# One opening block: setup, first norm and weight turns interleaved, and later weight loads held back behind wqk0

## The chip, the cores and the metric

The kernel runs on one core of a Trainium2 chip. The metric is the device time of one execution, in microseconds, as the median of several runs. A profiled execution of the same kernel gives the trace from which rows are read; "span" is the time from its first to its last instruction.

## What is computed

Four layers are applied to `x` (4 batches, 256 tokens, 128 features), each conditioned on one vector per batch. Layer 0, cut to what the change touches:

```python
mod = silu(c) @ W_mod + b_mod                 # six vectors of 128 per batch
sh_msa, sc_msa, g_msa, sh_mlp, sc_mlp, g_mlp = split(mod, 6)
h = layernorm(x) * (1 + sc_msa) + sh_msa
q, k, v = split(h @ W_qkv, 3)                 # 16 heads of 64
x = x + g_msa * (softmax(q k^T / 8) v @ W_out + b_out)
x = x + g_mlp * (gelu((layernorm(x) * (1 + sc_mlp) + sh_mlp) @ W1 + b1) @ W2 + b2)
```

Layer 1 is a graph attention over the edge tensor `adj`, layers 2 and 3 are attention blocks of 16 heads of 8 with modulated norms; layer 3 has an MLP. Activations are held transposed (features on the partitions), so a norm turns `x` with TensorE into token form, takes its statistics there, and turns it back.

## The kernel before

**The order of the work.** A planner at the top of the file writes a list of steps. Each step holds "heavy" ticks (`gv`: q, k and v of a batch in layer 0; `attention`) and "light" ticks (norms, projections, MLPs, layer 1). Every engine walks that one list in its own instruction stream, so the order on each engine is fixed when the kernel is built, and semaphores hold it where a producer is late. The list begins with the eight ticks of `norm 0a` of batch 0; then `gv` of batch 0 begins beside `norm 0a` of batch 1, and a step later attention of batch 0.

**Two blocks.** Ahead of the walk stands a block of setup (L504 to L584). SyncE (SP) issues every load of the beginning in one queue (L507 to L519): `vec`, the modulation columns of `w0`, `x` of batch 0, the two halves of `wqk0` (q and k weights, 512 KB each, into the tile `room`), `x` of batches 1 to 3, the rest of `w0`, `wbias`, `w1`, `w2`, `w3`, `bv2`. GpSimd (POOL) makes the identity and small constants (L531 to L538). ScalarE (ACT) and VectorE (DVE) form silu of the condition (L543, L558 to L560), TensorE (PE) multiplies it with the modulation columns (L583), and DVE makes the modulation vectors from that (L562 to L575). `vec` and the modulation columns share the semaphore `first_in`, so silu waits for both. All engines meet at the end of this block before the second one begins.

**The start of the second block.** SP goes on with the loads of `adj` (L702, L704). POOL makes the masks and zeroed tiles (L869 to L898) before it walks the list. PE turns `x` of batch 0 (L1378), DVE takes the statistics (L1075, L1079), ACT forms the reciprocal deviation (L908, L911), DVE normalizes (L1085), PE turns back (L1387) and ACT modulates into `hT` (L921). Then, in `gv` of batch 0, PE turns the 16 pieces of `wqk0` in four parts (L1397), ACT copies parts 0 and 2 out of PSUM (L928) and DVE parts 1 and 3 (L1104); two PSUM banks alternate. With all four copied, PE makes q and k of two heads at a time (L1406, "a G pair" below: two float32 matmuls, four matmul records), DVE copies them to `big` (L1111), ACT casts them to `room` (L933), and the scores follow (L1455). The v products (L1416) need the rest of `w0`; the late modulations (L1581) need `w1` to `w3` and `bv2`; the edge work on DVE (L1241) needs `adj`.

Of the kernel before, what the change touches and what calls it, by code (L numbers as in the profile page):

```python
# [383 lines left out]
def cond_seq_kernel(nc, x_t, adj, w0, wqk0, w1, w2, w3, wp2, wproj3, vecs, rows, out_t):  # L384
    with ExitStack() as ctx:
# [93 lines left out]
        first_in = sem("first_in")  # L479
# [13 lines left out]
        mods_full = sem("mods_full")  # L493
        w_full = sem("w_full")
# [5 lines left out]


        with nc.Block() as block:
            @block.sync
            def _(sp):  # L504

                mod0 = slice(*W0_AT["mod"])
                sp.dma_start(vec[:], vecs).then_inc(first_in, 16)  # L507
                sp.dma_start(w0s[:, mod0], w0[:, mod0]).then_inc(first_in, 16)
                sp.dma_start(xT[:, 0, :], x_t[0]).then_inc(x_loaded[0], 16)
                for s in range(2):  # L510
                    sp.dma_start(wqk0s[s * DH0:(s + 1) * DH0], wqk0[:, s]).then_inc(wqk_in, 16)
                for b in range(1, B):
                    sp.dma_start(xT[:, b, :], x_t[b]).then_inc(x_loaded[b], 16)
                sp.dma_start(w0s[:, mod0.stop:], w0[:, mod0.stop:]).then_inc(w0_in, 16)
                sp.dma_start(wbias[:], rows[0:1, D:D + NL + 1].broadcast_to([128, NL + 1])).then_inc(wbias_in, 16)
                sp.dma_start(w1s[:], w1).then_inc(weights_in, 16)
                sp.dma_start(w2s[:], w2).then_inc(weights_in, 16)
                sp.dma_start(w3s[:], w3).then_inc(weights_in, 16)
                sp.dma_start(bv2[:], rows[0:1, 0:D].broadcast_to([128, D])).then_inc(weights_in, 16)  # L519

            @block.gpsimd
            def _(pool):
                done = [0]

                def step(ins):

                    done[0] += 1
                    ins.then_inc(consts_step, 1)
                    pool.wait_ge(consts_step, done[0])

                step(nc.gpsimd.memset(ident[:], 0.0))  # L531
                step(nc.gpsimd.affine_select(out=ident[:], in_=ident[:], compare_op=ALU.not_equal, fill=1.0, base=0,
                                             pattern=[[-1, 128]], channel_multiplier=1))
                nc.gpsimd.tensor_copy(identb[:], ident[:]).then_inc(consts, 1)
                nc.gpsimd.memset(zero[:], 0.0)
                nc.gpsimd.memset(eps[:], EPS)
                nc.gpsimd.memset(lnd[:], -0.5 * math.log(D))
                nc.gpsimd.memset(ones[:], 1.0).then_inc(consts, 1)  # L538

            @block.scalar  # L540
            def _(act):
                act.wait_ge(first_in, 32)
                nc.scalar.activation(silu[:, 0, :], col(0, "cond", 0, B), ACT.Exp, scale=-1.0).then_inc(act_exp_c, 1)  # L543

            @block.vector
            def _(dve):
                done = [0]

                def step(ins):

                    done[0] += 1
                    ins.then_inc(setup_step, 1)
                    dve.wait_ge(setup_step, done[0])

                dve.wait_ge(first_in, 32)
                dve.wait_ge(act_exp_c, 1)

                step(nc.vector.tensor_scalar(silu[:, 1, :], silu[:, 0, :], 1.0, None, ALU.add))  # L558
                step(nc.vector.reciprocal(silu[:, 2, :], silu[:, 1, :]))
                nc.vector.tensor_tensor(silu[:, 0, :], silu[:, 2, :], col(0, "cond", 0, B), ALU.mult).then_inc(silu_ready, 1)  # L560
                dve.wait_ge(mods_full, 1)
                step(nc.vector.tensor_tensor(raw[:, 0:6, :], psum[:, 2, 0:6 * B].rearrange("p (c b) -> p c b", b=B),  # L562
                                             col(0, "mods", 0, 6).unsqueeze(2).broadcast_to([128, 6, B]), ALU.add))

                def block_mods(base, sc, sh, gate, bias):

                    nc.vector.tensor_scalar(mods_all[:, base, :], raw[:, sc, :], 1.0, None, ALU.add)
                    nc.vector.tensor_copy(mods_all[:, base + 1, :], raw[:, sh, :])
                    nc.vector.tensor_copy(mods_all[:, base + 2, :], raw[:, gate, :])
                    step(nc.vector.tensor_scalar(mods_all[:, base + 3, :], raw[:, gate, :], bias, None, ALU.mult))  # L570

                block_mods(SC0A, 1, 0, 2, col(0, "b_out0"))
                block_mods(SC0B, 4, 3, 5, col(0, "b2_0"))
                nc.vector.tensor_scalar(bq1s[:], col(0, "bq1", 0, 2), float(DH) ** -0.5, None, ALU.mult)
                nc.vector.tensor_tensor(bout1[:], col(0, "bout1", 0), col(0, "bout1", 1), ALU.add)  # L575

            @block.tensor
            def _(pe):
                pe.wait_ge(first_in, 32)
                pe.wait_ge(silu_ready, 1)  # L580
                for c in range(6):
                    at = W0_AT["mod"][0] + D * c
                    mm = nc.tensor.matmul(psum[:, 2, B * c:B * c + B], w0s[:, at:at + D], silu[:, 0, :],  # L583
                                          start=True, stop=True)  # L584
                mm.then_inc(mods_full, 1)
# [106 lines left out]
        with nc.Block() as block:  # L692
            @block.sync
            def _(sp):

                for b in range(B):
# [51 lines left out]
            def _(pool):  # L748
                zeros = [0]
# [85 lines left out]
                def norm(name, b):  # L835
# [66 lines left out]
            def _(act):  # L902
                def norm(name, b):
# [21 lines left out]
                def gv(b):  # L925
                    for n in range(0, W_PARTS if b == 0 else 0, 2):
                        act.wait_ge(w_full, n + 1)
                        nc.scalar.copy(w_heads(n), s_bank("W", n).rearrange("p (h s d) -> p s h d", s=2, d=DH0)  # L928
                                       ).then_inc(w_by_act, 1)
# [121 lines left out]
                nc.scalar.preload_act_table_set(EXP_LN_SET)  # L1051
# [3 lines left out]
            def _(dve):  # L1055
                xb_at = [0] * B

# [9 lines left out]
                def norm(name, b):  # L1067
# [21 lines left out]
                    xb_at[b] = n + 1  # L1089
                    for _ in range(FM_TICK - 2):  # L1090
# [10 lines left out]
                def gv(b):  # L1101
                    for n in range(1, W_PARTS if b == 0 else 0, 2):
# [257 lines left out]

                walk({"late mods": late_mods} | dict(norm=norm, gv=gv, attention=attention, project=project, mlp=mlp, edges=edges,
# [3 lines left out]
            def _(pe):  # L1365
                def done(ins, key):
                    ins.then_inc(work_full[W_BANK_OF[key]], 1)

                def norm(name, b):
# [10 lines left out]
                    done(ins, key)  # L1380
                    for _ in range(FM_TICK):
# [9 lines left out]
                def gv(b):  # L1391
                    if b == 0:
                        pe.wait_ge(wqk_in, 16 * 2)
                        for n in range(W_PARTS):
                            wait_s_bank_free(pe, "W", n)
                            for j in range(4):
                                ins = nc.tensor.transpose(s_bank("W", n)[:, j * 128:(j + 1) * 128],  # L1397
                                                          wqk0s[:, 4 * n + j, :], ident[:])
                            ins.then_inc(w_full, 1)
                        pe.wait_ge(w_by_act, W_PARTS // 2)  # L1400
                        pe.wait_ge(w_by_dve, W_PARTS // 2)
# [383 lines left out]
```

## Time and profile before

| what | value |
|---|---|
| median of 3 runs | 502.93 us (501.56 to 503.46) |
| profiled execution: its own time | 503.15 us |
| profiled execution: span | 501.4 us |
| TensorE busy | 412.6 us, 82% |
| VectorE busy | 309.7 us, 62% |
| ScalarE busy | 281.8 us, 56% |
| GpSimd busy | 175.4 us, 35% |
| mean granted TensorE clock | 0.969 |

The profiled execution took 1.75 us more than its span; that lies around the instructions. Busy shares are means over the whole span and say little of a short stretch, so the beginning is read from views of that stretch alone. In a timeline a line holds one or more instructions of one kind in a row: start, total length, engine, source line, operation, tile written and tiles read, count, and in brackets how long the engine sat idle before it and what ended that. A float32 matmul appears as two records.

### The profile page before, as it was taken

What the parts mean: (1) busy time and instruction counts of PE and PEld (TensorE: products, weight loads), DVE (VectorE), ACT (ScalarE), POOL (GpSimd) and SP (SyncE); (2) the same over time, 40 slices, a digit from 0 to 9 for tenths busy, and PEclk for the clock granted to TensorE, in tenths of its full rate; (3) what the DMA queues carried; (4) which work ended last, traced back from release to release, by engine and by line L of the source; (5) the groups of instructions that cost most, each with busy time, mean ns of one, the idle gap of its engine ahead of it and who ended that gap; (6) DMA issues with size and microseconds to landing.
All of it is one profiled execution on the core that took longest, in us unless ns stands there. A gap on an engine that the chain in (4) does not pass through costs nothing. (4 is left out here: it accounts for less than half of the span.)

```text
span 501.4 us, 9353 instructions
## 1 busy us (share of the span) xinstructions
PE 412.6 (82%) x3196; PEld 262.0 (52%) x3196; DVE 309.7 (62%) x846; ACT 281.8 (56%) x597; POOL 175.4 (35%) x226
## 2 busy tenths in 40 slices
PE   2777787988989999879996979778788889798974
PEld 2534454555646556445564546344455666576643
DVE  2464686864555646655376675776888777665721
ACT  2243254446545565445755586365767666668674
POOL 2812121331155331593369330641334322321200
PEclk9999899999999999999998899797999999899998
DMA  8920033000000000120002112001322313210000
GB/s 251 248 20 1 2 37 41 8 1 1 0 1 2 0 1 1 56 61 13 0 23 66 41 57 70 3 1 31 95 68 88 99 29 100 77 64 12 3 12 10
DMA packets 34527, 21.25 MB, mean 42 GB/s; under 512 B 22832, under 2 KB 31408, under 8 KB 34096
## 3 DMA queue, kind: packets, MB, share of 16 engines
q1 hardware_dynamic: 34480, 20.65, 15.8%
q8 instruction: 26, 0.43, 0.4%
q14 instruction: 21, 0.17, 0.1%
HBM read 16.97 MB, written 3.67 MB: 41 GB/s over the span
## 5 line engine op out<-in xcount | busy, mean ns | idle before, releaser
L965 ACT ACTIVATE pt<-psum 128x512 f32<-128x512 f32 (+1 forms) x192 | 106.1, 558 | 94.0 <-PE psum L1507 46.1
L1135 DVE TENSOR_REDUCE negm<-psum 128x2 f32<-128x512 f32 x128 | 84.5, 683 | 38.3 <-PE psum L1437 23.4
L760 POOL TENSOR_TENSOR pairsum<-pt 128x256 f32<-128x256 f32 x64 | 46.7, 730 | 141.1 <-ACT pt L965 137.7
L771 POOL COPY big<-mT 32x1024 bf16<-32x1024 bf16 x32 | 33.1, 1035 | 118.7 <-ACT mT L957 118.3
L1483 PE MATMUL psum<-big 128*128 128x256 bf16 (+1 forms) x256 | 50.3, 266 | 4.6 <-POOL big L771 3.4
L1132 DVE TENSOR_REDUCE negm<-psum 128x3 f32<-128x384 f32 x64 | 34.8, 554 | 16.8 <-PE psum L1443 16.1
L1502 PE MATMUL psum<-big 64*128 64x256 f32 x256 | 39.1, 396 | 2.4 <-ACT pt L965 2.2
L1176 DVE TENSOR_TENSOR oT<-psum,rden 128x256 f32<-128x256 f32 x64 | 26.5, 414 | 17.5 <-ACT rden L981 16.9
L1406 PE MATMUL psum<-hT,pt 128*128 128x256 f32 x128 | 34.8, 409 | 2.1 <-DVE negm L1135 1.2
L1531 PE MATMUL psum<-pt,room 128*64 128x256 f32 x256 | 36.5, 408 | 0.0
L1111 DVE COPY big<-psum 128x512 f32<-128x512 f32 x32 | 22.0, 689 | 20.3 <-PE psum L1406 20.1
L1531 PE MATMUL psum<-pt,vpad 128*32 128x256 f32 (+1 forms) x512 | 32.6, 374 | 1.6 <-DVE oT L1176 1.6
L1062 DVE SCALAR_TENSOR_TENSOR xT<-psum,mods_all,xb 128x256 f32<-128x256 f32 x20 | 9.7, 483 | 35.6 <-PE psum L1602 18.7
L1483 PEld LDWEIGHTS psum<-big 128*128 128x128 bf16 x256 | 24.0, 100 | 14.4 <-ACT pt L965 5.4
L1406 PEld LDWEIGHTS psum<-hT,pt 128*128 128x128 f32 x128 | 23.6, 198 | 10.7 <-issue 4.1
L1437 PE MATMUL psum<-big 72*128 72x256 bf16 x128 | 25.9, 285 | 3.5 <-DVE negm L1135 1.9
L845 POOL TENSOR_SCALAR xb<-xT,mods_all 128x256 f32<-128x256 f32 x24 | 22.2, 928 | 17.8 <-DVE xT L1062 16.5
L1441 PE MATMUL psum<-big 72*128 72x128 bf16 (+1 forms) x128 | 25.3, 249 | 3.5 <-DVE negm L1132 3.2
L933 ACT CAST room<-big 128x512 bf16<-128x512 f32 x32 | 19.1, 612 | 14.4 <-DVE big L1111 14.4
L1502 PEld LDWEIGHTS psum<-big 64*128 64x128 f32 x256 | 19.5, 186 | 12.7 <-ACT pt L965 5.5
L981 ACT ACTIVATE rden<-rden,zero 128x256 f32<-128x256 f32 x48 | 24.4, 508 | 1.6
L1443 PE MATMUL psum<-mask_qk,identb 128*128 128x128 bf16 x128 | 25.0, 220 | 0.0
(184 smaller groups left out, 859.8 us busy)
## 6 DMA issues: line engine op xcount, KB each, us to landing
big<-scratch SPq DMA_DIRECT2D x96, 96.0 KB
scratch<-room SPq DMA_DIRECT2D x48, 64.0 KB, 2.0
adj_s<-adj SPq DMA_DIRECT2D x16, 110.0 KB, 3.9
w0s<-w SPq DMA_DIRECT2D x1, 1536.0 KB, 9.6
w3s<-w SPq DMA_DIRECT2D x1, 1088.0 KB, 12.0
room<-wqk SPq DMA_DIRECT2D x2, 512.0 KB, 6.5
xT<-x_t SPq DMA_DIRECT2D x4, 128.0 KB, 6.5
w1s<-w SPq DMA_DIRECT2D x1, 512.0 KB, 9.9
```

What stands on the lines that cost most here:

```text
L760: nc.gpsimd.tensor_tensor(pairsum[:, u % SUM_RING, :], pt[:, pt_slot(u), 0:T], pt[:, pt_slot(u), T:2 * T], ALU.add).then_inc(pairsum_ready, 1)
L771: nc.gpsimd.tensor_copy(stacks[SHIFT_ROW:128, b % ROOMS, 0, GH * g:GH * (g + 1), :], mT[SHIFT_ROW:128, at % 2, :].unsqueeze(1).broadcast_t ...
L965: nc.scalar.activation(pt[:, pt_slot(u), 0:width], psum[:, ST_BANK + u % 2, 0:width], ACT.Exp, scale=EXP_SCALE[layer]).then_inc(pt_ready, 1)
L1132: ins = nc.vector.tensor_reduce(negm[:, g, :, j], bk[:, 0:384].rearrange("p (n k) -> p n k", n=NT + 1), AX_X, ALU.max, negate=True)
L1135: ins = nc.vector.tensor_reduce(negm[:, g, 0:NT, j], bk.rearrange("p (q k) -> p q k", q=NT), AX_X, ALU.max, negate=True)
L1176: nc.vector.tensor_tensor(oT[:, b % ROOMS, c, :], psum[:, O_BANK + o % 2, 0:T], rden[:, o % 2, :], ALU.mult).then_inc(o_done, 1)
L1406: ins = nc.tensor.matmul(s_bank("G", n, b)[:, s * T:(s + 1) * T], wqk0t[:, s, 128 * n:128 * (n + 1)], hT0[:, b % H_ROOMS], start=True, sto ...
L1437: ins = nc.tensor.matmul(bk[:, q * T:(q + 1) * T], lhs, keys, start=True, stop=True)
L1441: nc.tensor.matmul(bk[:, at:at + (q + 1) * 128], lhs, keys[:, 0:(q + 1) * 128], start=True, stop=False)
L1483: ins = nc.tensor.matmul(dst, lhs, rhs[:, q0:T], start=True, stop=(layer == 2))
L1502: nc.tensor.matmul(psum[:, ST_BANK + h % 2, k * T:(k + 1) * T], qk0[half, b % ROOMS, h // 2, 1, k * 128:(k + 1) * 128], qk0[half, b % ROOM ...
L1531: ins = nc.tensor.matmul(bk[at:at + m, qk:T], lhs, pt[:, pt_slot(u_base + h), k * T:(k + 1) * T - qk], start=(k == 0), stop=(k == NT - 1))
```

## The change

The first block is gone and its work is written into the second one.

- **Loads.** SP issues `vec`, then `x` of batch 0, then the modulation columns, then the two halves of `wqk0`. Then SP waits until both halves have landed, and only then issues all other loads, followed by those of `adj`. `vec` and the modulation columns have a semaphore each.
- **POOL** makes the identity and the constants, and goes straight on with masks and zeroed tiles. Its first `xb` waits for a new semaphore, `mods_ready`.
- **ACT** loads its function table first, forms the exponential for silu when `vec` is in, and in the norm of batch 0 copies parts 0 and 2 of the turned weights before it makes `hT`, which now waits for `mods_ready`.
- **DVE** forms silu first; in the norm of batch 0 it makes the modulation vectors between the statistics and the normalizing, and copies part 1 right behind the normalizing. Part 3 stays in `gv`.
- **PE** turns `x` of batch 0, multiplies the modulation columns, turns weight parts 0 to 2, then turns the normalized `x` back, and turns part 3 in `gv`. G pairs wait for the copy of the part that they read, not for all four.

The core of the diff (removed lines of the first block are moved unless shown otherwise):

```diff
-        first_in = sem("first_in")
+        vec_in = sem("vec_in")
+        mod_in = sem("mod_in")
+        mods_ready = sem("mods_ready")
...
             @block.sync
             def _(sp):
+                mod0 = slice(*W0_AT["mod"])
+                sp.dma_start(vec[:], vecs).then_inc(vec_in, 16)
+                sp.dma_start(xT[:, 0, :], x_t[0]).then_inc(x_loaded[0], 16)
+                sp.dma_start(w0s[:, mod0], w0[:, mod0]).then_inc(mod_in, 16)
+                for s in range(2):
+                    sp.dma_start(wqk0s[s * DH0:(s + 1) * DH0], wqk0[:, s]).then_inc(wqk_in, 16)
+
+                sp.wait_ge(wqk_in, 16 * 2)
+                for b in range(1, B):
+                    sp.dma_start(xT[:, b, :], x_t[b]).then_inc(x_loaded[b], 16)
+                sp.dma_start(w0s[:, mod0.stop:], w0[:, mod0.stop:]).then_inc(w0_in, 16)
...
             @block.gpsimd
                         pool.wait_ge(x_loaded[b], 16)
+                        pool.wait_ge(mods_ready, 1)
...
             @block.scalar
+                nc.scalar.preload_act_table_set(EXP_LN_SET)
+                act.wait_ge(vec_in, 16)
+                act.wait_ge(consts, 2)
+                nc.scalar.activation(silu[:, 0, :], col(0, "cond", 0, B), ACT.Exp, scale=-1.0).then_inc(act_exp_c, 1)
...
-                    for _ in range(FM_TICK - 1):
+                    for tick in range(FM_TICK - 1):
+                        if (name, b, tick) == ("0a", 0, 1):
+                            for part in range(0, W_PARTS, 2):
+                                act.wait_ge(w_full, part + 1)
+                                nc.scalar.copy(w_heads(part), s_bank("W", part).rearrange(...)).then_inc(w_by_act, 1)
                         yield
...
                     wait_full(act, fm)
+                    if name == "0a":
+                        act.wait_ge(mods_ready, 1)
...
             @block.vector
                         nc.vector.bn_aggr(mv[:, t, :], stats[:, t, :]).then_inc(mv_ready, 1)
+                    if (name, b) == ("0a", 0):
+                        first_mods()
...
                     xb_at[b] = n + 1
+                    if (name, b) == ("0a", 0):
+                        for part in range(1, W_PARTS - 1, 2):
+                            dve.wait_ge(w_full, part + 1)
+                            nc.vector.tensor_copy(w_heads(part), s_bank("W", part).rearrange(...)).then_inc(w_by_dve, 1)
...
+                silu_of_cond()
                 walk({"late mods": late_mods} | dict(norm=norm, gv=gv, attention=attention, ...
...
             @block.tensor
+                pe.wait_ge(consts, 2)
...
                         ins = nc.tensor.transpose(bank(key)[:, t * 128:(t + 1) * 128], xT[:, b, t * 128:(t + 1) * 128],
                                                   ident[:])
                     done(ins, key)
+                    if (name, b) == ("0a", 0):
+                        first_mods()
+                        for part in range(W_PARTS - 1):
+                            turn_weights(part)
...
                 def gv(b):
                     if b == 0:
-                        pe.wait_ge(wqk_in, 16 * 2)
-                        for n in range(W_PARTS):
...
-                        pe.wait_ge(w_by_act, W_PARTS // 2)
-                        pe.wait_ge(w_by_dve, W_PARTS // 2)
+                        turn_weights(W_PARTS - 1)
                     pe.wait_ge(h_ready, h_after("0a", b))
                     for n in range(H // 2):
+                        if b == 0 and n % 2 == 0:
+                            pe.wait_ge((w_by_act, w_by_dve)[n // 2 % 2], n // 4 + 1)
...
                         if u == 0:
                             pe.wait_ge(more_consts, 1)
+                            pe.wait_ge(mods_ready, 1)
```

`turn_weights(n)` waits for `wqk0` and for the PSUM bank, and makes the four transposes of part n; `first_mods` and `silu_of_cond` hold the moved instructions of the old block.

## Rows read from the trace of the kernel before

**Rows 1.** The page: span and number of instructions.
```profile
span 501.4 us, 9353 instructions
```

**Rows 2.** Waits of all engines up to 10.2 us: releaser, total, times, longest.
```profile
POOL sel L869 <- POOLq L502: 8.0, 1, 8.0
PE psum L583 <- DVE silu L560: 5.7, 1, 5.7
```

**Rows 3.** Timeline of the first block: start, length, engine, line, operation.
```profile
4.68 0.20 ACT L543 ACTIVATE silu<-vec 128x4 f32<-128x4 f32 x1 [2.60 <-DMA w0s<-w]
...
5.73 2.70 PE L583 MATMUL psum<-silu,w0s 128*128 128x4 f32 x12 [5.73 <-DVE silu L560]
...
9.71 0.15 DVE L575 TENSOR_TENSOR bout<-vec 128x1 f32<-128x1 f32 x1
```

**Rows 4.** Timeline from the second block's start to the first G pair.
```profile
10.17 0.66 PE L1378 MATMUL psum<-ident,xT 128*128 128x128 f32 x2 [1.74 <-PEq L502]
...
12.18 0.73 DVE L1085 TENSOR_SCALAR xn<-psum,mv,rstd 128x128 f32<-128x128 f32 x2 [0.60 <-ACT rstd L911]
...
13.51 3.89 PE L1397 MATMUL psum<-ident,room 128*128 128x128 f32 x16
13.76 0.56 ACT L921 ACTIVATE hT<-psum,mods_all 128x256 f32<-128x256 f32 x1 [1.61 <-PE psum L1387]
14.61 0.58 ACT L928 COPY pt<-psum 128x512 f32<-128x512 f32 x1 [0.29 <-PE psum L1397]
...
18.23 2.05 PE L1406 MATMUL psum<-hT,pt 128*128 128x256 f32 x4 [0.83 <-DVE pt L1104]
```

**Rows 5.** Timeline: SP's issues of x of batch 0, wqk0, x of the others.
```profile
1.70 0.43 SPq L509 DMA_DIRECT2D xT<-x_t  x1
...
2.17 1.20 SPq L511 DMA_DIRECT2D room<-wqk  x2
3.41 1.53 SPq L513 DMA_DIRECT2D xT<-x_t  x3
```

**Rows 6.** DMA issues, one short window each: count, KB, us from issue to landing.
```profile
vec<-vecs SPq DMA_DIRECT2D x1, 23.0 KB, 1.7
...
xT<-x_t SPq DMA_DIRECT2D x1, 128.0 KB, 3.3
...
room<-wqk SPq DMA_DIRECT2D x1, 512.0 KB, 5.5
...
room<-wqk SPq DMA_DIRECT2D x1, 512.0 KB, 7.4
...
bv<-rows SPq DMA_DIRECT2D x1, 64.0 KB, 12.1
```

**Rows 7.** Windows: busy time per engine, granted clock, DMA share, GB/s (last columns).
```profile
0.00:3.90 3.90, 0.00 (x0) 0.00 (x0) 0.00 (x0) 1.28 (x1) 1.18 (x11) 1.00 0.39 104
0.00:5.00 5.00, 0.00 (x0) 0.00 (x0) 0.00 (x0) 1.49 (x2) 1.18 (x11) 1.00 0.51 147
...
0.00:8.30 8.30, 2.57 (x12) 2.60 (x12) 0.51 (x3) 1.49 (x2) 1.18 (x11) 1.00 0.70 191
0.00:10.20 10.20, 2.73 (x13) 2.70 (x13) 1.81 (x14) 1.55 (x3) 1.25 (x12) 1.00 0.77 207
...
7.50:9.00 1.50, 0.93 (x5) 0.84 (x4) 0.50 (x5) 0.00 (x0) 0.00 (x0) 1.00 0.89 182
```

**Rows 8.** Timeline: first users of the loads that are held back.
```profile
33.56 1.10 PE L1416 MATMUL psum<-w0s,hT 128*128 128x512 f32 x2 [0.37 <-DVE big L1111]
...
56.57 0.61 DVE L1241 TENSOR_TENSOR room<-adj_s,wbias 128x440 f32<-128x440 int32 x1
```

**Rows 9.** Windows of line L1406 alone: PE and PEld busy, granted clock, DMA.
```profile
18.20:22.40 4.20, 3.89 (x8) 2.40 (x8) 1.00 1.02 132
24.40:28.70 4.30, 4.15 (x16) 2.77 (x16) 1.00 0.81 70
```

**Rows 10.** Window of PE alone: busy, granted clock, DMA share, GB/s.
```profile
56.00:60.00 4.00, 3.52 (x18) 0.57 0.02 4
```

More of the change, by code:

```diff
@@ L499, in col @@
             return vec[:, VEC_AT[name][0] + i:VEC_AT[name][0] + i + n]
[L502 to L585, printed above, removed]
@@ L694, in _ @@
             def _(sp):
+                mod0 = slice(*W0_AT["mod"])
[8 more added lines that the diff above has]
+                sp.dma_start(w0s[:, mod0.stop:], w0[:, mod0.stop:]).then_inc(w0_in, 16)
+                sp.dma_start(wbias[:], rows[0:1, D:D + NL + 1].broadcast_to([128, NL + 1])).then_inc(wbias_in, 16)
+                sp.dma_start(w1s[:], w1).then_inc(weights_in, 16)
+                sp.dma_start(w2s[:], w2).then_inc(weights_in, 16)
+                sp.dma_start(w3s[:], w3).then_inc(weights_in, 16)
+                sp.dma_start(bv2[:], rows[0:1, 0:D].broadcast_to([128, D])).then_inc(weights_in, 16)
                 for b in range(B):
@@ L748, in _ @@
             def _(pool):
+                nc.gpsimd.memset(ident[:], 0.0).then_inc(consts_step, 1)
+                pool.wait_ge(consts_step, 1)
+                nc.gpsimd.affine_select(out=ident[:], in_=ident[:], compare_op=ALU.not_equal, fill=1.0, base=0,
+                                        pattern=[[-1, 128]], channel_multiplier=1).then_inc(consts_step, 1)
+                pool.wait_ge(consts_step, 2)
+                nc.gpsimd.tensor_copy(identb[:], ident[:]).then_inc(consts, 1)
+                nc.gpsimd.memset(zero[:], 0.0)
+                nc.gpsimd.memset(eps[:], EPS)
+                nc.gpsimd.memset(lnd[:], -0.5 * math.log(D))
+                nc.gpsimd.memset(ones[:], 1.0).then_inc(consts, 1)
                 zeros = [0]
@@ L913, in norm @@
                         return
-                    for _ in range(FM_TICK - 1):
+                    for tick in range(FM_TICK - 1):
+                        if (name, b, tick) == ("0a", 0, 1):
+                            for part in range(0, W_PARTS, 2):
+                                act.wait_ge(w_full, part + 1)
+                                nc.scalar.copy(w_heads(part), s_bank("W", part).rearrange("p (h s d) -> p s h d", s=2, d=DH0)
+                                               ).then_inc(w_by_act, 1)
                         yield
@@ L925, in gv @@
                 def gv(b):
[L926 to L929, printed above, removed]
                     for n in range(H // 2):
@@ L1101, in gv @@
                 def gv(b):
-                    for n in range(1, W_PARTS if b == 0 else 0, 2):
+                    for n in range(W_PARTS - 1, W_PARTS if b == 0 else 0):
                         dve.wait_ge(w_full, n + 1)
@@ L1367, in done, with first_mods, turn_weights @@
                     ins.then_inc(work_full[W_BANK_OF[key]], 1)
+                pe.wait_ge(consts, 2)
+                def first_mods():
+                    pe.wait_ge(mod_in, 16)
+                    pe.wait_ge(vec_in, 16)
+                    pe.wait_ge(silu_ready, 1)
+                    for c in range(6):
+                        at = W0_AT["mod"][0] + D * c
+                        ins = nc.tensor.matmul(psum[:, 2, B * c:B * c + B], w0s[:, at:at + D], silu[:, 0, :],
+                                               start=True, stop=True)
+                    ins.then_inc(mods_full, 1)
+                def turn_weights(n):
+                    pe.wait_ge(wqk_in, 16 * 2)
+                    wait_s_bank_free(pe, "W", n)
+                    for j in range(4):
+                        ins = nc.tensor.transpose(s_bank("W", n)[:, j * 128:(j + 1) * 128], wqk0s[:, 4 * n + j, :], ident[:])
+                    ins.then_inc(w_full, 1)
                 def norm(name, b):
```

30 lines of the change are left out of this document (24 added, 6 removed).

## The prediction

> **What bounds the kernel now.** I read the page first. The span is 501.4 us [rows 1], and the change touches only its beginning, so whole-span shares decide nothing; what counts is when TensorE's long run of dependent work begins. I take the first G pair (L1406) as that point: everything after it follows the planned order, and it starts at 18.23 us, released by DVE's last copy of turned weights [rows 4]. Then I read the waits up to 10.2 us: PE had nothing for 5.7 us, until silu was there, and POOL stood 8.0 us at the end of the first block [rows 2]. The timeline gives the reasons. Silu's exponential needs only `vec`, but ran at 4.68, when the modulation columns had landed [rows 3]. PE made the modulations from 5.73 to 8.43, DVE ended its vectors at 9.86 [rows 3], and only behind the block's end, at 10.17, was `x` turned [rows 4]. The chain then was turn, statistics, normalize, turn back, 16 weight pieces from 13.51, G at 18.23 [rows 4]. Last I read the loads: landing is issue plus the time in the DMA view. `x` of batch 0 landed at 1.70 + 3.3 = 5.0, the second half of `wqk0` at 2.8 + 7.4 = 10.2 (second issue of the pair) [rows 5, 6]. So `x` lay ready for 5 us and `wqk0` for 3.3 us before PE used them. These two waits are what can go.
>
> **The change, part by part.** The sum runs to the new start of the first G pair.
>
> *Front end.* `vec` lands 1.7 us after the first issue, about 2.5 us; silu took 4.68 to 5.58, 0.9 us, so it is ready near 3.4 [rows 3, 6]. The modulation columns and `x` of batch 0 swap places in the queue; the bytes ahead of the later one are the same, so I put the columns at 5.0, where `x` landed. `x` lands between 3.0 (issued one issue of 0.43 earlier, 1.27, plus the 1.7 of `vec`) and 4.6 (1.27 plus its old 3.3) [rows 5, 6]. Turning it takes 0.66 [rows 4] and ends by 5.3. Then PE multiplies the columns, 2.70 us, to about 7.8; DVE's vectors take 8.43 to 9.86, 1.4 us, to 9.2; the normalizing, now behind them on DVE, 0.73, to 10.0 [rows 3, 4]. Statistics and deviation (from 10.83, the end of that turn, to 12.18, where the normalizing began) run beside the multiplication. ACT loaded its table before `vec` landed in the old kernel too; the table load of the second block goes, but was hidden behind the statistics: nothing.
>
> *wqk0.* This is the term that the trace does not show, because the old queue never paused. Through `wqk0` the queue carries 23 + 384 + 128 + 1024 KB, 1.60 MB in decimal units. By 8.3 us 191 GB/s had moved 1.59 MB, by 10.2 us 207 GB/s had moved 2.11 MB [rows 7]. So about 0.5 MB of later transfers went by before `wqk0` was in. Lower bound: all slots go to `wqk0`, the bytes are moved at 8.3, and landing comes 0.7 us behind the bytes (by 3.9 us 104 GB/s had moved 0.41 MB, as much as `vec` and the columns hold, and the columns were waited for until 4.68) [rows 3, 7]: 9.0. Upper bound: from 5.0, when 147 GB/s had moved 0.74 MB, the remaining 0.86 MB go at the lowest rate nearby, 182 GB/s [rows 7], 4.7 us, plus 0.7: 10.4. I take 9.6, inside but nearer the old landing of 10.2, since the DMA engines were 0.89 busy at that low rate, so other transfers were perhaps not its only brake.
>
> *A rule against it.* The old trace shows 0.5 MB overtaking. The Trainium skill, page "DMA: Bandwidth & Descriptors", section "Queues, rings and completion order", says that each DMA engine consumes the descriptors of a queue in issue order, which speaks against the holding back: later loads would stand behind `wqk0` anyway. By that rule nothing is gained from the hold; here the byte count in the rows disagrees with a strict reading, though the page also allows a later transfer to finish first. What it would give is priced as the third rival.
>
> *Weights and norm.* PE turns part 0 when `wqk0` is in and the multiplication is done, so `wqk0` decides (9.6 against 7.8). The 16 pieces took 3.89 us, 0.97 a part; an ACT copy of 0.58 fits beside the next part [rows 4], so part 2 finds its bank free. The path is three parts (2.9), the turn back (0.66), part 3 (0.97), 4.55 us, plus 0.15 for handovers. ACT's copy of part 2 (0.58) lies beside the turn back and `hT` (0.56) beside part 3: hidden, with 0.3 us to spare. The last DVE copy, which released the first G pair before, is now only needed by the second bank and later pairs, and lies beside the first pair. First G pair: 9.6 + 4.55 + 0.15 = 14.3 us. The gain is 18.23 - 14.3 = 3.9 us; by the bounds of `wqk0` 3.1 to 4.5.
>
> *SP.* Behind its new wait stand `x` of batches 1 to 3, the rest of `w0`, `wbias`, `w1` to `w3`, `bv2` and `adj`: the issues shift from 3.41 to about 9.7, 6.3 us. `x` of batch 1, with the 3.3 us of batch 0, lands near 13; PE wants it behind the first G pair, at 16.4. `w0` and the rest: even the longest landing, 12.1 us [rows 6], from a last issue at 14 (three at 1.53 together and six more like them from 9.7) gives 26; the v products start at 33.56 - 3.9 = 29.7, the edges at 52.7, the late modulations between them [rows 5, 8]. `adj`, issued behind these, has 26 us more. All hidden. *POOL* no longer stands 8.0 us at the block's end [rows 2]; it was not on the path. Its new wait for the modulations at 9.2 comes behind masks that end later than that: nothing.
>
> *Behind the first G pair* the engines keep their order, so I carry the 3.9 us to the end. One thing may add to it. The 8 records of the first two G pairs took 3.89 us, 0.49 each, later ones 4.15 for 16, 0.26 [rows 9]; the granted clock reads 1.00 (the 2.4 GHz level) in both windows, so that column does not show what slows the first ones. I take it that the first pairs stay slow, since the work ahead of them is the same in length; the other end is a rival.
>
> *Sum.* Span 501.4 - 3.9 = 497.5; with 1.75 around it 499.25; the profiled execution lies 0.2 above the median of the runs: **499.0 us**. What a measurement of this kernel can tell from no change is about 0.5%, 2.5 us, so under 500.4 is faster.
>
> **The rivals.**
>
> *TensorE in its faster form from the start.* PE now works nearly without a pause from 5 us. If the first two G pairs ran at 0.26 (8 x 0.23 = 1.8 us) and the weight pieces gained in proportion (3.89 x 0.4, 1.5 us), the gain is 7.2: 495.7. For: the old pauses between 8.4 and 13 go. Against: pieces and G pairs were slow through 13.51 to 22.4, nine mostly busy microseconds [rows 4, 9].
>
> *The start is given back to the clock.* From 56 to 60 us the granted clock was 0.57 of full, so the 1.2 GHz level held for 3.4 us and lost at most 1.7 [rows 10]. Two more such drops leave 3.9 - 3.4 = 0.5 us: 502.4, no change. For: the row shows that such stretches occur, and not what would keep them where they are. Against: order and gaps behind the start are the same, so drops may also vanish.
>
> *The hold buys nothing.* If the 0.5 MB of later transfers moved only in slots that `wqk0` could not use, it lands at 10.2 as before; first G pair at 14.9, gain 3.3: 499.6. Only the merging of the blocks pays. The order rule of the page above comes out here.
>
> *The held loads become the bound (slower).* SP's wait stands ahead of `x` of batch 1, which PE turns between the first two G pairs in fixed order. It costs something from the point where it lands after 16.4, takes the whole gain at 20.3, and ends 2.5 us slower (505.4) at 22.8, which needs 13 us from issue to landing. Against: the longest landing in a full queue is 12.1 [rows 6], and now the queue is empty before it.
>
> **How the numbers follow.** Forecast 0.56, all of it faster. Faster form 0.12, faster. Hold buys nothing 0.12, of which 0.10 counts as faster, since it lies only 0.8 us inside the bound. Given back 0.15, no change. Held loads 0.05, slower. Faster 0.78, same 0.17, slower 0.05. The range runs from 496.0 (the faster form short of its full price; early `wqk0` alone is 498.4) to 501.2 (one drop of 1.7 on top of the late `wqk0`, 499.8, reaches 501.5); it leaves out about 2 in 10.
>
> **What would show it.** Right: `x` turned by 5.3, mod vectors done near 9.2, weight part 0 released by the DMA of `wqk0` between 9.0 and 10.4, first G pair at 13.7 to 15.1, and v products, late modulations and edges each about 3.9 us earlier, none waiting for a DMA. Wrong: a first G pair later than 16, PE waiting for `x` of batch 1, G records of 0.26 from the first pair, or steps at 100 us shifted by much less than the first G pair.

## The result and the profile after

The changed kernel took 499.01 us (median of 22 runs, 495.53 to 504.58) where the kernel before took 502.51 (22 runs, 499.77 to 507.28) beside it: a ratio of 0.9937, with a 95% interval of 0.9919 to 0.9956. The ratio is that of the medians without the one run of each kernel that lies more than 1.5% above its fastest, 499.00 and 502.19, so the gain is 3.2 us, 2.2 to 4.1 by the interval. The profiled execution took 498.17 us.

The page of the changed kernel, its span [rows 1]:

```profile
span 496.4 us, 9353 instructions
```

The timeline of its beginning, TensorE and what it waits for, answers to [rows 3, 4]; line numbers are those of the changed file (L1386 turns `x` and L1399 turns it back, L1365 makes the modulations, L1374 turns weights, L1412 are the G pairs, L1422 the v products of [rows 8]).

```profile
3.51 0.66 PE L1386 MATMUL psum<-ident,xT 128*128 128x128 f32 x2 [3.51 <-DMA xT<-x_t]
...
5.33 2.72 PE L1365 MATMUL psum<-silu,w0s 128*128 128x4 f32 x12 [1.16 <-DMA w0s<-w]
...
9.20 0.54 DVE L1031 COPY mods_all<-raw 128x4 f32<-128x4 f32 x1
...
9.97 2.97 PE L1374 MATMUL psum<-ident,room 128*128 128x128 f32 x12 [1.92 <-DMA room<-wqk]
...
10.31 0.72 DVE L1066 TENSOR_SCALAR xn<-psum,mv,rstd 128x128 f32<-128x128 f32 x2
...
12.74 0.63 PE L1399 MATMUL psum<-ident,xn 128*128 128x128 f32 x2
...
13.16 1.06 PE L1374 MATMUL psum<-ident,room 128*128 128x128 f32 x4
...
14.09 1.44 PE L1412 MATMUL psum<-hT,pt 128*128 128x256 f32 x4
...
15.58 1.03 PE L1412 MATMUL psum<-hT,pt 128*128 128x256 f32 x4
...
28.06 1.10 PE L1422 MATMUL psum<-w0s,hT 128*128 128x512 f32 x2 [0.37 <-DVE big L1097]
```

PE now starts at 3.5, and each of its first three stages is released by a transfer. The weights are released by `wqk0` at 9.97, and the first G pair starts at 14.09 instead of 18.23: 4.1 us. At the first v product the lead is 33.56 - 28.06 = 5.5 us. The other 1.4 us lie in the first two G pairs, whose windows answer to [rows 9] (PE busy, PEld busy, granted clock, DMA share, GB/s):

```profile
14.05:16.65 2.60, 2.46 (x8) 1.60 (x8) 1.00 1.01 397
18.80:23.10 4.30, 4.20 (x16) 2.79 (x16) 1.00 0.97 396
```

Eight records took 2.46 us, not 3.89: only the first few are still slow. Below, "slow form" means the pace of 0.49 us for such a record (0.24 for a weight piece), "faster form" that of 0.26 (0.13). The issues of `wqk0`'s halves (KB, us to landing) and four windows of DMA traffic answer to [rows 6, 7]:

```profile
room<-wqk SPq DMA_DIRECT2D x1, 512.0 KB, 5.5
...
room<-wqk SPq DMA_DIRECT2D x1, 512.0 KB, 7.1
```

```profile
0.00:8.30 8.30, 3.38 (x14) 2.93 (x14) 1.95 (x8) 1.99 (x4) 6.17 (x21) 1.00 0.76 187
8.30:10.00 1.70, 0.03 (x1) 0.03 (x1) 1.62 (x9) 0.00 (x0) 1.46 (x4) 1.00 0.13 24
...
8.60:8.80 0.20, 0.00 (x0) 0.00 (x0) 0.20 (x3) 0.00 (x0) 0.14 (x2) 1.00 0.24 41
8.80:10.00 1.20, 0.03 (x1) 0.03 (x1) 1.13 (x6) 0.00 (x0) 1.06 (x3) 1.00 0.00 0
```

The second half, issued near 2.8, landed at 9.9; it was 10.2 before. These windows count a DMA packet, bytes and time, where the packet starts. So by 8.3 us packets of 1.55 of the 1.60 MB had started, and the last one started before 8.8. A packet of 8 KB takes 0.6 us here; by the packet records of the trace the last one runs from 8.74 to 9.34. The bytes were in at 9.34, and the landing followed 0.6 us later, close to the 0.7 of the prediction. What came later than its lower bound is the end of the bytes: 9.34, not 8.3.

How the lead travels is read from DVE's first update of `x` after the first attention of layer 0, one row each for the kernel before and the changed one:

```profile
104.00 0.48 DVE L1062 SCALAR_TENSOR_TENSOR xT<-psum,mods_all,xb 128x256 f32<-128x256 f32 x1 [3.15 <-PE psum L1602]
```

```profile
98.31 0.48 DVE L1041 SCALAR_TENSOR_TENSOR xT<-psum,mods_all,xb 128x256 f32<-128x256 f32 x1 [3.16 <-PE psum L1609]
```

The lead is 5.7 us there and 5.0 at the end of this pair of profiles, while the runs together give 3.2. The difference is taken up with the repeated profiles.

### The profile page after: what moved, and what is told of

It reads as the page before. It is cut to its first block and busy times, and to the rows that moved or that the text cites. A ratio compares the mean times of both kernels' runs of the same rounds, so it can differ in the third digit from the quotient of the medians.

```text
span 496.4 us, 9353 instructions
## 1 busy us (share of the span) xinstructions
PE 410.4 (83%) x3196; PEld 261.3 (53%) x3196; DVE 310.9 (63%) x846; ACT 280.1 (56%) x596; POOL 175.7 (35%) x226
## 5 line engine op out<-in xcount | busy, mean ns | idle before, releaser
L1509 PE MATMUL psum<-big 64*128 64x256 f32 x256 | 40.1, 404 | 2.5 <-ACT pt L917 2.4
L1412 PE MATMUL psum<-hT,pt 128*128 128x256 f32 x128 | 33.3, 396 | 1.4 <-DVE negm L1121 1.3
L1489 PEld LDWEIGHTS psum<-big 128*128 128x128 bf16 x256 | 24.1, 100 | 14.3 <-ACT pt L917 5.4
L1412 PEld LDWEIGHTS psum<-hT,pt 128*128 128x128 f32 x128 | 22.8, 192 | 9.7 <-issue 5.1
```

Source lines behind the costliest of these rows:

```text
L1412: ins = nc.tensor.matmul(s_bank("G", n, b)[:, s * T:(s + 1) * T], wqk0t[:, s, 128 * n:128 * (n + 1)], hT0[:, b % H_ROOMS], start=True, sto ...
L1489: ins = nc.tensor.matmul(dst, lhs, rhs[:, q0:T], start=True, stop=(layer == 2))
L1509: nc.tensor.matmul(psum[:, ST_BANK + h % 2, k * T:(k + 1) * T], qk0[half, b % ROOMS, h // 2, 1, k * 128:(k + 1) * 128], qk0[half, b % ROOM ...
```

## The experiments

All runs are in one table; "v" is the start of the first v product, "x update" that of the DVE row just shown, both from the run's timeline. Times and ratios are given where more than one run was made; the ratio is to the kernel before on the same chip.

| run | first G pair | v | x update | span | mean clock | median us | ratio (95%) |
|---|---|---|---|---|---|---|---|
| before | 18.23 | 33.56 | 104.00 | 501.4 | 0.969 | | |
| after | 14.09 | 28.06 | 98.31 | 496.4 | 0.965 | 499.01 | 0.9937 (0.9919 to 0.9956) |
| e1_no_hold | 14.21 | 27.87 | 98.23 | 495.7 | 0.969 | 499.76 | 0.9925 (0.988 to 0.9969) |
| e2_hold_alone | 23.77 | 38.41 | 107.41 | 507.0 | 0.969 | 507.47 | 1.0105 (1.002 to 1.019) |
| e3_turns_late | 16.99 | 31.63 | 106.25 | 504.7 | 0.946 | 503.25 | 1.0008 (0.9968 to 1.0049) |
| e4_warm | 14.07 | 27.86 | 98.10 | 496.7 | 0.962 | 499.93 | 0.9926 (0.9877 to 0.9976) |
| b_again | 18.28 | 33.26 | 105.22 | 502.9 | 0.966 | | |
| a_again | 14.33 | 28.71 | 101.29 | 500.4 | 0.959 | 500.21 | 0.9893 (0.9852 to 0.9933) |
| a_third | 14.35 | 28.74 | 101.30 | 500.6 | 0.959 | 498.47 | 0.9882 (0.9833 to 0.9931) |
| b_fill | 16.72 | 31.36 | 106.04 | 503.9 | 0.952 | | |
| e5_masks_later | 14.13 | 27.80 | 99.69 | 498.5 | 0.966 | | |
| e6_split | 12.66 | 26.35 | 96.59 | 494.2 | 0.965 | | |
| e7_split_masks | 12.14 | 25.81 | 97.71 | 496.5 | 0.965 | 497.62 | 0.9857 (0.9826 to 0.9888) |
| e7_again | 12.39 | 26.41 | 96.66 | 495.3 | 0.966 | 497.57 | 0.9878 (0.9827 to 0.9929) |

**e1_no_hold: the changed kernel without the hold.**

```diff
                     sp.dma_start(wqk0s[s * DH0:(s + 1) * DH0], wqk0[:, s]).then_inc(wqk_in, 16)
-
-                sp.wait_ge(wqk_in, 16 * 2)
                 for b in range(1, B):
```

> The changed kernel without SP's wait for wqk0. Theory A (the hold buys almost nothing; wqk0 lands 1.6 us behind its last bytes whatever follows it): second half of wqk0 lands at 10.2 instead of 9.9, first G pair at 14.4 instead of 14.1, first v product at 28.4 instead of 28.1, time within 0.5% of the changed kernel and so about 0.7% under the kernel before. Rival B (the hold carries the gain, by taking 0.5 MB out of the way): wqk0 at 11 or later, first G pair at 15.2 or later, at least 1 us of the start lost.

The issue of the second half, and PE's release, in its profile:

```profile
room<-wqk SPq DMA_DIRECT2D x1, 512.0 KB, 7.3
```

```profile
10.10 2.97 PE L1372 MATMUL psum<-ident,room 128*128 128x128 f32 x12 [2.12 <-DMA room<-wqk]
```

`wqk0` is waited for until 10.10 instead of 9.97, the first G pair starts 0.1 us later, and the ratio is the changed kernel's. Theory A holds as to the gain: the hold carries nothing that can be told from the spread, since the two repeats of the changed kernel, with the hold, were released at 10.22 and 10.24. Its 1.6 us behind the last bytes is a misreading (see above); here the last packet of `wqk0` ends at 9.23 and the landing follows 0.8 us later.

The reason can be read from the kernel before, from its start to the start of the last packet of `wqk0`:

```profile
0.00:8.65 8.65, 2.70 (x12) 2.64 (x12) 0.69 (x4) 1.49 (x2) 1.18 (x11) 1.00 0.72 193
```

By then packets of 1.67 MB had started, 1.60 of them up to and with `wqk0`. So only 0.07 of the 0.5 MB of later transfers had begun ahead of its last packet; the rest moved while that packet ran, until 9.24, and while the landing was still to come, until 10.2. They were behind `wqk0` and not in its way. The Trainium skill, page "DMA: Bandwidth & Descriptors", section "Queues, rings and completion order", says that each DMA engine consumes the descriptors of a ring in order; the trace agrees to within the 0.07 MB.

**e2_hold_alone: the kernel before with the hold.**

```diff
                 for s in range(2):
                     sp.dma_start(wqk0s[s * DH0:(s + 1) * DH0], wqk0[:, s]).then_inc(wqk_in, 16)
+                sp.wait_ge(wqk_in, 16 * 2)
                 for b in range(1, B):
```

> The kernel before with SP's wait alone. Theory A (there wqk0 was never the last to come): first G pair stays at 18.2, first v product at 33.6, time the same within 0.5%. Rival B (the hold itself gains): first G pair earlier by 0.3 us or more. Rival C (held loads become the bound): x of batch 1 or the v products waited for, first v product later than 34.

None of the three came: the v product was later than 34, as rival C had it, but not by waiting for a held load. Its timeline around the end of the first block, and its first G pair:

```profile
10.79 1.29 SPq L514 DMA_DIRECT2D xT<-x_t  x3
...
15.06 0.67 SPq L520 DMA_DIRECT2D bv<-rows  x1
...
16.17 0.66 PE L1379 MATMUL psum<-ident,xT 128*128 128x128 f32 x2 [8.01 <-PEq L502]
...
23.77 1.10 PE L1407 MATMUL psum<-hT,pt 128*128 128x256 f32 x4 [0.83 <-DVE pt L1105]
```

SP issues the held loads one after the other from 10.79 to 15.73, and only then does the first block end for every engine. PE sat idle for 8.0 us with `x` landed. The v product is 4.9 us late and the time rises by 1.05%. The hold did not bring `wqk0` in earlier either: SP went on at 10.79, and it landed at 10.2 and 10.8 in the two profiles of the kernel before. So the hold is harmless only because the change also takes the blocks apart: a wait on SP inside a block that all engines must leave is a wait for all of them.

**e3_turns_late: the blocks merged, the weights turned behind the norm as before.** The loop of `turn_weights` moves from `norm` into `gv`, the copies of ACT and DVE with it, and G waits for all four copies.

```diff
                         first_mods()
-                        for part in range(W_PARTS - 1):
-                            turn_weights(part)
...
-                        turn_weights(W_PARTS - 1)
+                        for part in range(W_PARTS):
+                            turn_weights(part)
+                        pe.wait_ge(w_by_act, W_PARTS // 2)
+                        pe.wait_ge(w_by_dve, W_PARTS // 2)
```

> The changed kernel with all four weight parts turned behind the norm again, and copied in gv, as before. Theory A (merging the blocks and turning early each carry about half): the norm ends near 12.3, parts turned from 11.7, first G pair at 16.3, that is 1.9 us of the 4.1 from merging and 2.2 from the order; first v product near 30.3 if G pairs get faster as early, 31.7 if not. Rival B (merging alone does it): first G pair at 14.5 or earlier. Rival C (order alone): first G pair at 17.8 or later.

```profile
12.65 3.51 PE L1368 MATMUL psum<-ident,room 128*128 128x128 f32 x16
...
16.99 1.10 PE L1405 MATMUL psum<-hT,pt 128*128 128x256 f32 x4 [0.83 <-DVE pt L1084]
```

The first G pair at 16.99 lies between the rivals, nearest to theory A: 1.2 us from merging and 2.9 from the order. In this run the modulation columns came 1.6 us later than in the changed kernel (PE made the modulations from 6.90), and vectors, normalizing and turn back follow one another from there; without it, by estimate (16.99 - 1.6), merging would have about 2.8 us and the order 1.3. Yet nothing is left in the time: 1.0008. In the profile the lead of 1.9 us at the v product is a delay of 2.3 at the update of `x`. Between them the granted clock was low, 0.79 in this run against 0.96 in the kernel before (window of PE alone: busy, granted clock, DMA share, GB/s):

```profile
20.00:60.00 40.00, 30.09 (x152) 0.79 0.33 66
```

```profile
20.00:60.00 40.00, 28.65 (x167) 0.96 0.19 18
```

This profiled run took 506.49 us, the longest of the ten, so the profile shows where its own time went and not why the median gained nothing. That stays open.

**e4_warm: the changed kernel with PE's three pauses filled.**

```diff
+                def busy(times):
+                    for _ in range(times):
+                        nc.tensor.transpose(psum[:, O_BANK, 0:128], ident[:], ident[:])
+
+                busy(5)
...
+                        busy(4)
                         first_mods()
+                        busy(7)
                         for part in range(W_PARTS - 1):
```

> The changed kernel with 5, 4 and 7 extra transposes of the identity (results unused) in TensorE's three pauses before x, before the modulation columns and before wqk0. Theory A (how long PE has been busy sets when matmuls run in the faster form): the 12 weight pieces of parts 0 to 2 take 1.6 to 2.2 us instead of 2.97, first G pair near 13, both first G pairs at about 1.05 us instead of 1.44 and 1.03, first v product 1 to 1.5 us earlier than 28.1. Rival B (something else sets it, such as the time since the start): pieces stay at 0.24 each, first G pair at 14.1, first pairs as before.

```profile
9.96 2.97 PE L1380 MATMUL psum<-ident,room 128*128 128x128 f32 x12 [0.43 <-DMA room<-wqk]
...
14.07 1.25 PE L1420 MATMUL psum<-hT,pt 128*128 128x256 f32 x4
```

The twelve pieces took 2.97 us as before, so rival B has the pieces right; the first G pair took 1.25 us instead of 1.44, but e1 and e5 show 1.13 without any extra work, and the repeats below 1.83 and 1.85. Here the filling bought nothing that can be told.

**b_again, a_again, a_third: both kernels once more, unchanged.**

> The kernel before, unchanged, profiled once more. Theory A (when PE's faster form begins varies from run to run, and the first profile of the kernel before was a late case, 22.2 us, 9 us after sustained work began, where the other five profiles show 3 to 5 us): the faster form begins between 16 and 19 us, first G pair at 17.0 to 18.2, first v product at 31.5 to 32.5 instead of 33.6. Rival B (fixed by this kernel's order): again at 22, first v product at 33.5.

> The changed kernel, unchanged, profiled and timed again. The order of its beginning is fixed, so wqk0 lands at 9.7 to 10.3 and the first G pair starts at 13.5 to 14.5; the first v product at 27.5 to 28.5. Time 0.6 to 0.7% under the kernel before, as in its first comparison.

> The changed kernel, timed once more beside the version with split wqk0. Theory: first G pair at 14.1 to 14.4, time 0.6 to 1.0% under the kernel before.

```profile
18.28 2.04 PE L1406 MATMUL psum<-hT,pt 128*128 128x256 f32 x4 [0.83 <-DVE pt L1104]
...
33.26 1.10 PE L1416 MATMUL psum<-w0s,hT 128*128 128x512 f32 x2 [0.37 <-DVE big L1111]
```

The kernel before repeats its beginning: rival B. Its first G pairs were slow in both profiles. The changed kernel repeats the landing and the first G pair (14.33 and 14.35), but its first two pairs took longer, so v came at 28.7, later than expected, and in both repeats a low clock follows (0.57, near the 1.2 GHz level, which reads 0.50) that the first profile does not have there. The same stretch and the same v products, first in the first profile, then in a_third:

```profile
32.00:40.00 8.00, 5.00 (x32) 1.00 0.20 15
...
33.27 1.98 PE L1422 MATMUL psum<-w0s,hT 128*128 128x512 f32 x4 [0.77 <-DVE negm L1121]
```

```profile
32.00:40.00 8.00, 6.01 (x18) 0.57 0.24 20
...
34.07 3.78 PE L1422 MATMUL psum<-w0s,hT 128*128 128x512 f32 x4 [0.75 <-DVE negm L1121]
```

The four records took 1.8 us longer, and behind them a_third keeps the delay up to the update of `x`:

```profile
101.30 0.48 DVE L1041 SCALAR_TENSOR_TENSOR xT<-psum,mods_all,xb 128x256 f32<-128x256 f32 x1 [3.16 <-PE psum L1609]
```

The update of `x` comes at 101.3 there, 3.0 us later than in the first profile. The repeat of the kernel before has such a stretch too, a clock of 0.79 from 36 to 44 us, and its update comes at 105.22, 1.2 us later than in its first profile although its v product came 0.3 earlier. So a stretch of low clock moves what follows by 1.5 to 2.3 us here, in either kernel, and the lead at the update of `x` is anything from 2.7 to 6.9 us, at the end of the span from 0.8 to 6.5, by the pair of profiles that is taken. A single pair does not give the gain.

The ratios of the repeats, 0.9893 and 0.9882, are lower than the first and than either expectation, but rest on 4 and 6 runs, and the intervals overlap. Both profiled repeats were the longest runs of theirs (502.18 and 502.28). A least-squares fit of time against mean granted clock, with a constant for each chip and each kernel, over 79 runs (the kernel before, the changed one, e1 and both e7), gives 2.5 us for each 0.01 of mean clock, and puts the changed kernel 4.6 us (95%: 3.7 to 5.6) and e1 3.8 us under the kernel before at equal clock. In these runs the mean clock of the changed kernel, 0.965, is no lower than that of the kernel before, 0.964 on the same chips. So the clock accounts for much of the difference between profiles, but that it takes a part of the gain on the average is not shown. No clocks are on record for the kernel before in the first comparison; why that gave 3.2 and these runs 4.6 stays open.

**b_fill: the kernel before with PE's pauses filled.**

```diff
                 mm.then_inc(mods_full, 1)
+                pe.wait_ge(consts, 2)
+                for _ in range(5):
+                    nc.tensor.transpose(psum[:, O_BANK, 0:128], ident[:], ident[:])
...
                     done(ins, key)
+                    if (name, b) == ("0a", 0):
+                        for _ in range(7):
+                            nc.tensor.transpose(psum[:, O_BANK, 0:128], ident[:], ident[:])
...
                             ins.then_inc(w_full, 1)
+                        for _ in range(3):
+                            nc.tensor.transpose(psum[:, O_BANK, 0:128], ident[:], ident[:])
```

> The kernel before with 5, 7 and 3 extra transposes of the identity (results unused) in TensorE's three pauses ahead of the first G pair (behind the modulations, behind the turn of x, and behind the weight pieces). Theory A (PE's pauses keep the first G pairs in the slow form): a faster form by 19 us, first G pair at 18.2 as before, first two pairs together under 3.2 us instead of 3.5 to 3.9, first v product at 31.5 to 32.5 instead of 33.3 to 33.6. Rival B (pauses do not matter): first v product at 33.0 or later.

```profile
13.34 1.04 PE L1403 MATMUL psum<-ident,room 128*128 128x128 f32 x8
14.63 1.26 PE L1403 MATMUL psum<-ident,room 128*128 128x128 f32 x8 [0.26 <-ACT pt L931]
...
16.72 1.10 PE L1414 MATMUL psum<-hT,pt 128*128 128x256 f32 x4 [0.50 <-DVE pt L1107]
```

Theory A, and stronger than expected: already the weight pieces run at 1.04 for 8, 0.13 each instead of 0.24, and the first G pair starts 1.5 us early. Only PE's pauses were filled, so in this kernel the filling changes the form in which the first pairs run. That pauses as such keep them slow does not follow: in e2_hold_alone PE stood idle for 8.0 us before it turned `x` and nothing was filled, and its first two pairs took 1.10 and 1.03 us. The lead of 2.2 us at the v product is gone at the update of `x` (106.04): the granted clock was 0.78 from 20 to 60 us.

**e5_masks_later: POOL's masks behind the modulation vectors.**

```diff
+                pool.wait_ge(mods_ready, 1)
                 step(nc.gpsimd.memset(sel[:], 0.0))
```

> The changed kernel with POOL's masks and zeroed tiles begun only behind the modulation vectors. Theory A (DVE's small operations run longer beside POOL's work): the DVE run from the first modulation addition to the last takes 1.4 us as in the kernel before instead of 2.3, normalizing starts near 9.5 instead of 10.3; first G pair unchanged at 14.1, since wqk0 decides. Rival B (something else slows them, such as arriving transfers): still 2.3 us.

```profile
8.93 0.16 DVE L1032 COPY mods_all<-raw 128x4 f32<-128x4 f32 x1
...
9.48 0.73 DVE L1067 TENSOR_SCALAR xn<-psum,mv,rstd 128x128 f32<-128x128 f32 x2
```

Theory A: the copy that took 0.54 us beside POOL's work takes 0.16, the vectors 1.4 us instead of 2.3, and the normalizing starts at 9.48 instead of 10.31. The first G pair stays at 14.1, since `wqk0` decides.

**e6_split, e7_split_masks, e7_again: wqk0 in two halves by heads, without and with the later masks.**

```diff
-                for s in range(2):
-                    sp.dma_start(wqk0s[s * DH0:(s + 1) * DH0], wqk0[:, s]).then_inc(wqk_in, 16)
+                for half in range(2):
+                    heads = slice(half * H // 2, (half + 1) * H // 2)
+                    for s in range(2):
+                        sp.dma_start(wqk0s[s * DH0:(s + 1) * DH0, heads], wqk0[:, s, heads]).then_inc(wqk_half[half], 16)
...
-                    pe.wait_ge(wqk_in, 16 * 2)
+                    pe.wait_ge(wqk_half[n // 2], 16 * 2)
```

> The changed kernel with wqk0 loaded in two halves by heads (four transfers of 256 KB, each half with its own semaphore) and POOL's masks behind the modulation vectors. Theory A (the landing of wqk0, not its bytes or PE, sets the first G pair): the first half lands near 7.7, parts 0 and 1 are turned from 8.1, part 2 from 10.0, first G pair at 12.5, first v product at 26.5, time about 1.5 us (0.3%) under the changed kernel. Rival B (the first half lands no earlier than 9.5, because completion waits on the whole queue): first G pair at 13.7 or later, no gain.

> The changed kernel with wqk0 loaded in two halves by heads, and POOL's masks where the change has them. Theory A (the split landing carries the whole gain of the pair of edits, since PE is the bound behind it): first G pair at 12.1 to 12.5, first v product at 25.8 to 26.5; DVE's modulation vectors take 2.3 us again and normalizing starts near 10.4, still in time for the turn back at 11. Rival B (the slower DVE now decides): PE waits for the normalized x, first G pair at 13 or later.

> The version with split wqk0 and later masks, timed once more beside the changed kernel. Theory: first G pair at 12.1, time 1.5 to 2.5 us under the changed kernel, 1.1 to 1.4% under the kernel before.

The beginning of e7_split_masks:

```profile
8.05 2.95 PE L1378 MATMUL psum<-ident,room 128*128 128x128 f32 x12
10.79 0.63 PE L1403 MATMUL psum<-ident,xn 128*128 128x128 f32 x2
...
12.14 1.13 PE L1416 MATMUL psum<-hT,pt 128*128 128x256 f32 x4
```

Theory A: PE goes from the modulations into the weights at 8.05 with no wait for a transfer, and the first G pair starts at 12.14, 2.0 us before the changed kernel's. In e6_split, where the masks stay early, it is 12.66, between its two theories: PE turns back at 11.19 what DVE has normalized by 11.04, so the slower DVE costs about 0.4 of the 0.5 us once `wqk0` no longer decides; 0.1 is the second half, for which part 2 waited until 10.01. The repeat e7_again, whose modulation columns came 0.2 later, started its first pair at 12.39, so 0.4 is not far above the spread. Both medians, 497.62 and 497.57, lie under those of the changed kernel on the same chips, 500.21 and 498.47; the differences, 2.6 and 0.9 us, were expected at 1.5 and at 1.5 to 2.5; the ratios' intervals overlap, so the size is open, and in the fit above it is 2.1 us at equal clock. Of the versions that ran more than once it is the fastest; e6_split ran once, in 495.94.

## Why the prediction was right

The account of what bound the beginning was right: `x` and `wqk0` lay landed while PE waited, taking the blocks apart and turning the weights early used that time, and the first G pair moved by 4.1 us where 3.9 were forecast. That 499.0 met 499.01 to the last digit is luck: several terms were off and made up for each other, and the kernel before itself came at 502.51 where the sum started from 502.9.

- **Front end.** Right. `x` was turned by 4.17 us (by 5.3 forecast), the modulations made from 5.33 to 8.05 (to 7.8). The vectors were done at 10.4, not 9.2: DVE's small operations were slowed by POOL's masks, which the change moved beside them (e5). The prediction had called POOL's new start free. It cost nothing, since the turn back came at 12.74; in e6 it did.
- **wqk0.** Landing at 9.9, inside the bounds of 9.0 and 10.4, 0.3 above the value taken. The 0.7 us between bytes and landing, worked out from the first loads, came out at 0.6; the bytes were in at 9.34, where the lower bound had 8.3 (its windows count packets where they start) and the value taken 8.9. The reason given for an early landing was wrong: the 0.5 MB were read as overtaking `wqk0`, but all except 0.07 MB of them moved behind its last packet, so there was nothing to keep away, and the byte count did not speak against the order rule. The rival that the hold buys nothing was the true account of this term; its price, a first G pair at 14.9, was too high (14.21 in e1).
- **Weights and norm.** 14.09 - 9.97 = 4.1 us where 4.55 + 0.15 were summed: the parts took 0.99 (2.97 for three), but part 3 began 0.42 us behind the start of the turn back, so their ends and starts overlapped and no handover was left. With `wqk0` late by 0.4 and this path short by 0.6, the first G pair came at 14.09 for 14.3.
- **The first G pairs "stay slow, since the work ahead of them is the same in length".** This step failed: 2.46 us for 3.89, 1.4 gained (1.0 in the repeats, where they took 2.86 and 2.88). Filling the pauses of the old kernel does the same (b_fill), but e2 has the faster form behind a longer pause, so what decides it stays open. The rival of the faster form had the effect in part; its weight pieces stayed slow.
- **"I carry the 3.9 us to the end".** As a sum it came out: 3.2 us were measured, 2.2 to 4.1, and 3.9 lies inside. The way there was another. The lead at the v product was already 4.5 to 5.5 us over the pairs of profiles (33.26 and 33.56 against 28.06 to 28.74), and behind it single profiles gained or lost with the stretches of low clock, in both kernels. The rival had priced one stretch at 1.7 us; a_third lost about 2.3 in its own (its update of `x` is 3.0 late, 0.7 of it before the v product). That such stretches took the rest of the lead on the average is not shown.
- **The held loads.** Never a bound: `x` of batch 1 was issued at 9.94 and was turned at 15.36 straight behind the first pair, and the v products waited for DVE, not for `w0`; late modulations (43.42 for 48.93) and edges (51.07 for 56.57) came 5.5 us earlier without waiting for a DMA. The danger lay elsewhere: with the old blocks the hold costs 4.9 us (e2).

## What to carry to other kernels

At a kernel's start, write down for each load when it lands and for each engine when it first could work on it; the gain here was in two loads that lay landed for 3 and 5 us, and not in the transfer that was made to hurry. Split a late load so that work can begin on its first part (2.0 us here), and keep every waiting issue out of a block that all engines must leave together. A lead of 1% at the start is not yet a lead at the end: repeat the profile, compare the granted clock of the stretch behind it, and take the gain from many runs. Before counting bytes in a window, ask whether it counts them where a packet starts or where it ends.

## What the runs showed of the hardware

- A transfer's landing lags its bytes: the last packet of `wqk0` ended at 9.34 and the landing came 0.6 us later; in the other profiles of both kernels and in e1 it was 0.6 to 1.0. The Trainium skill, page "DMA: Bandwidth & Descriptors", section "Anatomy of one DMA", puts a fixed cost of about 2 us mostly down to the wait for the write to be confirmed (for transfers that GpSimd issues; these are SP's). The 0.6 to 1.0 us here are less than half of that; how much of such a wait lies inside a packet's 0.6 us, no run here shows.
- Later transfers of the same queue did not slow an earlier one: `wqk0` released PE at 9.97, 10.22 and 10.24 with the later ones held back and at 10.10 without (e1).
- DVE operations on 128 x 4 elements took up to 0.54 us beside POOL's fills and selects, and 0.16 without (e5), 2.3 us instead of 1.4 over the run of eleven. The Trainium skill, page "SBUF — State Buffer", section "SBUF: two separate sides", says that DVE and GpSimd share one pair of ports, which a GpSimd operation or some kinds of DVE operation hold for a whole instruction; e5 agrees that POOL's work beside them is the cause; which operations are held up, and why only some, no run here shows.
- The same float32 work ran at half the pace in the first stretch: pieces at 0.24 us against 0.13, G records at 0.49 against 0.26, with a granted clock of 1.00 in the windows throughout. Filling the pauses moved the change of pace from about 22 us to about 12 in the old kernel (b_fill), and the pieces of the new one stayed slow with it (e4). Without filling it came at 11.4 (e7_split_masks) to 15.8 (a_again) in the new order, and at 21.7 in e2. What the engine must have done for it stays open; so does what sets off the stretches of low granted clock between 20 and 60 us, behind which the lead of the e3 and b_fill profiles was gone.
